# Routed experts in half blocks of two experts side by side, with outputs scattered to a row per choice

## The reference, cut to what matters

```python
def step(y, p):
    w1, b1, w2, b2, w3, b3, ge = p
    h = jax.nn.silu(xt @ w1 + b1) * (xt @ w2 + b2)
    return (y + ge[:, None] * (h @ w3 + b3), None)
y, _ = jax.lax.scan(step, jnp.zeros_like(xt), (ew1, eb1, ew2, eb2, ew3, eb3, gate.T))
z = jax.nn.silu(xt @ sw1 + sb1) * (xt @ sw2 + sb2) @ sw3 + sb3
return (y + z).reshape(shape)
...
x = x + jnp.tanh(g_ffn[0]) * _L0_ffn_ref(_layernorm(x, axis=-1), ...)
```

## Time and profile before

| | us |
|---|---|
| Time, median of 3 runs | 962.04 (961.36 to 962.27) |
| The profiled execution, its own time | 963.37 |
| Its span, first to last instruction | 961.6 |
| PE busy in it | 944.8 |
| DVE busy | 642.8 |
| ACT busy | 410.9 |
| POOL busy | 273.0 |

### The profile page before, as it was taken

The page is one execution under the profiler, slowest core; times in us unless marked ns, Lnnn a source line. Parts: engine busy times, 40 slices in busy tenths (PEclk is TensorE's granted clock), DMA queues, the critical chain, the costliest instruction groups (busy, mean ns, idle before and its releaser), DMA issues.

```text
span 961.6 us, 14022 instructions
## 1 busy us (share of the span) xinstructions
PE 944.8 (98%) x4863; PEld 790.2 (82%) x4863; DVE 642.8 (67%) x1074; ACT 410.9 (43%) x1004; POOL 273.0 (28%) x251
## 2 busy tenths in 40 slices
PE   9999999999999999999999999999999999999996
PEld 7888888888888788888888988989889887777773
DVE  6977679766665864643777778787787777843333
ACT  6336554333333342314556455464554425324442
POOL 1253434433433033003223122121311012043353
PEclk9999999999999999999999999999999999999998
DMA  7654554646456635548747636546465049565579
GB/s 265 223 206 177 187 196 154 229 166 217 174 210 202 217 146 202 202 153 308 262 168 294 225 137 229 197 168 225 138 227 187 39 165 346 197 206 184 171 199 262
DMA packets 86275, 193.75 MB, mean 201 GB/s; under 512 B 8608, under 2 KB 29344, under 8 KB 84800
## 3 DMA queue, kind: packets, MB, share of 16 engines
q1 hardware_dynamic: 76000, 171.64, 50.1%
q0 software_dynamic: 4272, 12.58, 5.0%
q10 hardware_dynamic: 5936, 8.65, 2.5%
HBM read 121.74 MB, written 71.11 MB: 201 GB/s over the span
## 4 chain that ended last, share of the span: by engine, by line
PE 89%; DVE 4%; DMA 2%; issue 2%; POOL 1%; ACT 0%; POOLq 0%; SPq 0%; DVEq 0%; ACTq 0%
PE ps_job L825 7%; PE ps_job L827 7%; PE ps_job L826 7%; PE ps_attn L1041 6%; PE ps_score L1013 6%; PE ps_attn L1285 4%; PE ps_turn L1027 3%; PE ps_score L885 3%; PE ps_score L887 3%; PE ps_score L886 3%; PE ps_attn L885 3%; PE ps_attn L886 3%; PE ps_attn L887 3%; PE ps_job L885 2%; PE ps_job L887 2%; PE ps_job L886 2%
## 5 line engine op out<-in xcount | busy, mean ns | idle before, releaser
L751 POOL TENSOR_TENSOR score_bias<-mask_bias,pos_bias 128x1024 f32<-128x1024 f32 x32 | 78.2, 2445 | 292.0 <-DVE probs L1855 185.9
L1339 ACT ACTIVATE probs<-probs,neg_max 128x128 f32<-128x128 f32 x256 | 99.4, 392 | 95.6 <-DVE neg_max L1858 95.6
L712 POOL TENSOR_TENSOR w_sum<-w_raw 128x256 f32<-128x256 f32 x30 | 22.6, 752 | 178.2 <-PE ps_score L887 72.3
L1041 PE MATMUL ps_attn<-pT,v_s 128*128 128x128 f32 x512 | 62.7, 276 | 1.3 <-issue 1.1
L1285 PE MATMUL ps_attn<-ew_s,xbT 128*128 x248 | 62.4, 380 | 0.9 <-ACT xbT L1329 0.9
L1013 PE MATMUL ps_score<-kq_s 128*128 128x128 f32 x512 | 62.4, 275 | 0.0
L1041 PEld LDWEIGHTS ps_attn<-pT,v_s 128*128 128x128 f32 x512 | 59.8, 192 | 2.0 <-issue 1.2
L1285 PEld LDWEIGHTS ps_attn<-ew_s,xbT 128*128 128x128 f32 x248 | 44.6, 190 | 20.1 <-issue 15.0
L1013 PEld LDWEIGHTS ps_score<-kq_s 128*128 128x128 f32 x512 | 59.9, 192 | 0.2
L1882 DVE TENSOR_TENSOR acc<-ps_job,acc 128x512 f32<-128x512 f32 x56 | 37.9, 685 | 29.9 <-PE ps_job L827 29.9
L783 POOL DMA_INDIRECT xb<-x_rows,token_of x31 | 31.2, 1007 | 84.8 <-ACT y_out L1600 40.2
(11 more groups left out here) (468 smaller groups left out, 2593.8 us busy)
## 6 DMA issues: line engine op xcount, KB each, us to landing
kq<-st SPq DMA_DIRECT2D x32, 1024.0 KB, 4.2
kq_s<-kq SPq DMA_DIRECT2D x64, 512.0 KB, 4.5
v_s<-v_all SPq DMA_DIRECT2D x8, 2048.0 KB, 10.8
w_raw<-wa_dram SPq DMA_DIRECT2D x31, 512.0 KB, 5.6
v_all<-st SPq DMA_DIRECT2D x24, 512.0 KB, 3.7
y_slots<-ones SPq DMA_DIRECT2D x32, 256.0 KB, 4.6
wo_raw<-wo_dram SPq DMA_DIRECT2D x8, 1024.0 KB, 6.9
ew_s<-ew_dram SPq DMA_DIRECT2D x4, 2048.0 KB, 12.6
```

The source lines that it names most:

```text
L751: nc.gpsimd.tensor_tensor(score_bias[:], mask_bias[:], pos_bias[:, i % 2].unsqueeze(1).broadcast_to([P, B, P]), ALU.add).then_inc(bias_rea ...
L1041: last = nc.tensor.matmul(ps_attn[half][:, cols(b)], v_s[g % 2][:, BH * half + b, cols(j)], pT[:, half, cols(b)], start=True, stop=True)
L1339: last = nc.scalar.activation(probs[i % 2][:, half, b], probs[i % 2][:, half, b], ACT.Exp, bias=neg_max[:, i % 2, half, b:b + 1], accum_ou ...
```

## The change

Blocks become pairs of half blocks. Each expert's slots are rounded up to 64 instead of 128. NHB = 47 half blocks can occur at most, so the loop runs NB = 24 times, and the two halves of a pair can belong to two experts. `block_h` makes eight products instead of four: for each chunk, one with 64 of the columns of `xbT` into the PSUM partitions 0 to 63, against `ew12_s`, and one with the other 64 into the partitions 64 to 127, against a copy `w12_b` of the second expert's weights. `block_y` makes two products in the same manner, the second one against a copy `w3_b`. DVE makes both copies (1024 and 512 columns) in every pair, loads two owners, and adds the bias in two instructions of 64 partitions.

PE's order for one b is `turn_x(b + 1)`, `turn_h(b - 2)`, `block_h(b)`, `block_y(b - 2)`; `block_h(b)` waits for `hb_biased` of b - 1, which was b - 2.

The gates leave `x_rows`, and ACT's copy to `y_out` (now 4 buffers) has no scale. POOL scatters each pair to `y_rows` in DRAM by an indirect DMA (`store_y`), to a row for each choice and token, so that SP can read them back by 8 plain loads of 512 KB (`y_back`) once the real pairs are stored. DVE multiplies by the gates in the last sums: 16 instructions of 512 columns in place of 4 adds of 1024. The gates `gate_f` are made by four instructions between `add_shared(1)` and `ended`. The clearing stores go.

```diff
-NB = (TOP * T + E * (P - 1)) // P
-NS = NB + 1
+HB = P // 2
+NHB = (TOP * T + E * (HB - 1)) // HB
+NB = (NHB + 1) // 2
+NS = 32
 XB = 11
+YB = 4
...
+        y_out += [place(f"y_out{n}", [P, D], F32, at_attn + (n - 2 + XB - XB_FIRST) * D * 4) for n in range(2, YB)]
...
+        y_back = place("y_back", [P, B, TOP, D], F32, at_ctx_hi)
+        assert TOP * B * D <= (E // 2) * W12
+        w3_b = [place(f"w3_b{n}", [P, D], F32, at_qk + SH * (2 * W12 + 8) * 4 + n * D * 4) for n in range(2)]
...
+        w12_b = [place(f"w12_b{n}", [P, C, 2 * P], F32, at) for n, at in enumerate((at_rt, at_b3))]
...
+        y_rows = nc.dram_tensor("y_rows", (3 * T + NS * P, D), F32, kind="Internal").ap()
+        y_row_tiles = y_rows[0:4 * T].rearrange("(n q t p) d -> q t p n d", n=TOP, q=2, t=B)[0]
...
-                sp.dma_start(y_slot_blocks[s].rearrange("p (c k) -> p c k", c=C),
-                             ones[:].unsqueeze(1).broadcast_to([P, C, P])).then_inc(cleared, 16)
...
-            sp.wait_ge(gates_out_ready, 1)
-            sp.dma_start(x_rows[:, D:].rearrange("(b p) e -> p b e", p=P), gates_out[:]).then_inc(x_rows_in, 16)
...
+            sp.wait_ge(stores_known, 1)
+            stored_blocks = [sp.value_load(stores_i[0:1, k:k + 1], min_val=HB, max_val=16 * ((NB + YB - 1) // YB))
+                             for k in range(YB)]
+            for k in range(YB):
+                sp.wait_ge(y_stored[k], stored_blocks[k])
             for t in range(B):
-                sp.wait_ge(final_ready, t // 2 + 1)
+                sp.dma_start(y_back[:, t], y_row_tiles[t]).then_inc(y_in[t], 16)
+            for t in range(B):
+                sp.wait_ge(final_ready, t + 1)
                 sp.dma_start(out[t], acc[:, t]).then_inc(stored, 16)
...
-            for b in range(NB):
+            for b in range(XB):
                 if b == XB_FIRST:
                     pool.wait_ge(shared_psum, B)
-                if b >= XB:
-                    pool.wait_ge(yb_sbuf, b - XB + 1)
                 load_x(b)
...
-            pool.wait_ge(stores_known, 1)
-            stores = [pool.value_load(stores_i[0:1, k:k + 1], min_val=P, max_val=16 * NB) for k in range(2)]
-            for k in range(2):
-                pool.wait_ge(y_stored[k], stores[k])
-            nc.gpsimd.tensor_tensor(slot_at[:], base_i[:], row_i[:], ALU.add).then_inc(rank_done, 1)
-            pool.wait_ge(shared_added, B)
-            pool.wait_ge(rank_done, 15)
-            def pick_up(n, t):
+            def store_y(b):
+                if b == 0:
+                    pool.wait_ge(token_ready, 2)
+                pool.wait_ge(yb_sbuf, b + 1)
                 nc.gpsimd.indirect_dma_start(
-                    out=(acc[:, t] if n else y_pick[t // BH][:, t % BH]), out_offset=None, in_=y_slots,
-                    in_offset=bass.IndirectOffsetOnAxis(ap=slot_at[:, n * B + t:n * B + t + 1], axis=0),
-                    bounds_check=NB * P - 1, oob_is_err=True,
-                    compute_op=(ALU.add if n else ALU.bypass)).then_inc(y_pick_in[t], 16)
-            for t in range(B):
-                for n in range(TOP):
-                    pick_up(n, t)
+                    out=y_rows, out_offset=bass.IndirectOffsetOnAxis(ap=row_of[:, b:b + 1], axis=0),
+                    in_=y_out[b % YB][:], in_offset=None,
+                    bounds_check=3 * T + NS * P - 1, oob_is_err=False).then_inc(y_stored[b % YB], 16)
...
-            def block_h(b, e, chunks):
+                return pe.value_load(owner[0:1, 2 * b:2 * b + 1], min_val=0, max_val=E - 1)
+            def block_h(b, e):
                 k = b % 2
-                for c in chunks:
-                    last = nc.tensor.matmul(ps_attn[k][:, 0:2 * P], xbT[k][:, cols(c)], ew12_s[:, e, c],
-                                            start=(c == 0), stop=(c == C - 1))
-                return last
+                for c in range(C):
+                    for half, w in enumerate((ew12_s[:, e, c], w12_b[k][:, c])):
+                        last = nc.tensor.matmul(ps_attn[k][half * HB:(half + 1) * HB, 0:2 * P], xbT[k][:, cols(2 * c + half, HB)],
+                                                w, start=(c == 0), stop=(c == C - 1))
+                last.then_inc(hb_psum, 1)
             def block_y(b, e):
                 k = b % 2
                 pe.wait_ge(hbT_sbuf, b + 1)
                 if b >= 2:
                     pe.wait_ge(yb_sbuf, b - 1)
-                nc.tensor.matmul(ps_job[k][:], hT_b[k][:], w3_s[:, e], start=True, stop=True).then_inc(yb_psum, 1)
+                for half, w in enumerate((w3_s[:, e], w3_b[k][:])):
+                    last = nc.tensor.matmul(ps_job[k][half * HB:(half + 1) * HB, :], hT_b[k][:, cols(half, HB)], w,
+                                            start=True, stop=True)
+                last.then_inc(yb_psum, 1)
...
-            turn_x(1)
             pe.wait_ge(shared_added, B)
-            owners = [owner_of(0)]
-            for b in range(NB):
-                pe.wait_ge(xbT_sbuf, b + 1)
+            owners = []
+            for b in range(NB + 2):
+                if b + 1 < NB:
+                    turn_x(b + 1)
                 if b >= 2:
-                    pe.wait_ge(hb_biased, b - 1)
-                if b == 0:
-                    block_h(b, owners[b], range(C)).then_inc(hb_psum, 1)
-                else:
-                    block_h(b, owners[b], range(2))
-                    turn_h(b - 1)
-                    block_h(b, owners[b], range(2, C)).then_inc(hb_psum, 1)
-                if b + 1 < NB:
-                    owners.append(owner_of(b + 1))
-                if b + 2 < NB:
-                    turn_x(b + 2)
-                if b == 1:
+                    turn_h(b - 2)
+                if b < NB:
+                    owners.append(owner_of(b))
+                    pe.wait_ge(xbT_sbuf, b + 1)
+                    if b >= 1:
+                        pe.wait_ge(hb_biased, b)
+                    block_h(b, owners[b])
+                if b == 2:
                     pe.wait_ge(ew3_in, 16 * 4)
-                if b >= 1:
-                    block_y(b - 1, owners[b - 1])
-            turn_h(NB - 1)
-            block_y(NB - 1, owners[NB - 1])
+                if b >= 2:
+                    block_y(b - 2, owners[b - 2])
...
+                if b >= YB:
+                    act.wait_ge(y_stored[b % YB], 16 * (b // YB))
+                copy(y_out[b % YB][:], ps_job[k][:]).then_inc(yb_sbuf, 1)
+            take_xbT(0)
+            for b in range(NB + 2):
+                if b + 1 < NB:
+                    take_xbT(b + 1)
+                if b < NB:
+                    k = b % 2
+                    act.wait_ge(hb_biased, b + 1)
+                    nc.scalar.activation(silu_b[k][:], h_b[k][:, 0:P], ACT.Silu).then_inc(silu_b_done, 1)
                 if b >= 2:
-                    act.wait_ge(y_stored[k], 16 * (b // 2))
-                nc.scalar.activation(y_out[k][:], ps_job[k][:], ACT.Copy,
-                                     scale=xb[b % XB][:, bass.ds(owners[b] + D, 1)]).then_inc(yb_sbuf, 1)
-                if b == 0:
-                    act.wait_ge(cleared, 16 * NS)
-                act.wait_ge(yb_sbuf, b + 1)
-                act.dma_start(y_slot_blocks[b], y_out[k][:]).then_inc(y_stored[k], 16)
-            def owner_of(b):
-                return act.value_load(owner[0:1, b:b + 1], min_val=0, max_val=E - 1)
-            take_xbT(0)
-            take_xbT(1)
-            act.wait_ge(owner_ready, 1)
-            owners = [owner_of(0)]
-            for b in range(NB):
-                k = b % 2
-                act.wait_ge(hb_biased, b + 1)
-                nc.scalar.activation(silu_b[k][:], h_b[k][:, 0:P], ACT.Silu).then_inc(silu_b_done, 1)
-                if b + 2 < NB:
-                    take_xbT(b + 2)
-                if b >= 1:
-                    take_y(b - 1)
-                if b + 1 < NB:
-                    owners.append(owner_of(b + 1))
-            take_y(NB - 1)
+                    take_y(b - 2)
...
-            dve.wait_ge(gain_done, 1)
-            V.scalar_tensor_tensor(out=gates_out[:], in0=masks[:], scalar=gain[:, 1:2], in1=scores[:],
-                                   op0=ALU.mult, op1=ALU.mult).then_inc(gates_out_ready, 1)
...
+            chain(V.tensor_scalar(blocks_i[:], ps_score[1][:, B * E:(B + 1) * E], float(HB - 1), None, ALU.add))
+            chain(V.tensor_scalar(blocks_i[:], blocks_i[:], HB.bit_length() - 1, None, ALU.arith_shift_right))
...
-            V.tensor_scalar(base_i[:], slot_i[:], -P, None, ALU.bitwise_and)
...
-            V.tensor_copy(token_of[:], ps_turn[1][:, 0:NS]).then_inc(token_ready, 1)
+            chain(V.tensor_copy(row_of[:], ps_turn[1][:, 0:NS]))
+            V.tensor_scalar(token_of[:], row_of[:], T - 1, None, ALU.bitwise_and).then_inc(token_ready, 1)
+            chain(V.scalar_tensor_tensor(out=spare[:], in0=ps_turn[1][:, 0:NS], scalar=0.0, in1=spare[:],
```

(62 more changed lines are left out.)

104 lines of the change are left out of this document (50 added, 54 removed).

## The result

The changed kernel took 955.81 us (median of four runs, 955.19 to 956.83), the kernel before 961.94 beside it: a ratio of 0.9938, with a 95% interval of 0.9921 to 0.9955. A second set gave 0.9944 (0.993 to 0.9958), 959.31 against 964.46.

What follows compares the result with a forecast made beforehand. The prediction took PE to bound the old loop and DVE the new one: first `h_b` 858.5 + pairs 81.7 + 0.8 + slow loads 2.7 + 2.55 + sums 11.2 + ending 2.9 = 960.3 profiled, 960.7 as median; range 948 to 977.

Steps and rivals of the forecast that it cites:

- 23 pairs: Loop after the first `h_b`: each pair takes 3.55 us, set by DVE, 81.7 us in all.
- slow loads in the ending: About pairs 21 and 22: four owner loads slowed by plain-load DMA traffic, some 0.7 us extra each, +2.7 us.
- last `h_b`, drain: End of loop: last bias 0.8 us, then DVE's remaining work before the sums, 2.55 us.
- part 3: Before the loop: `gate_f`, longer `ended` and `owner_f`, and first copies move the first `block_h` from 854.37 to 856.5, +2.1 us.
- part 1: PE in the loop: 24 pairs replace 31 blocks, both halves run at once, so a pair needs 3.14 us.
- the serial rival: `block_h` and `block_y`: halves run one after the other, PE needs 5.71 us a pair, total 1009; chance 0.17.
- part 2: DVE in the loop: owner loads, copies, two biases and handoffs sum to 3.5 us a pair, taken as 3.55.
- The bound moves from PE to DVE: Loop: DVE's 3.55 us a pair exceeds PE's 3.14, so 24 pairs cost 85 us, not 75.
- the third rival: Loop: DVE's owner loads hide, a pair takes PE's 3.14 to 3.3 us, total 948 to 952; chance 0.22.
- The collision: Loop: DVE's loads and copies collide with POOL's scatter, a pair takes 4.0 to 4.2 us, total 970 to 975; chance 0.21.
- break-even: Loop: if DVE and POOL collide, the changed kernel loses from a pair of 3.63 us on.
- part 4: Ending: 2.55 us on DVE, 16 sums of 11.2 (+6.6 on the path), last store and end 2.9; plain loads hidden.

Runs made afterwards that it cites:

- the shared ending: Changed kernel with owner loads made a pair ahead, plus two of the eight last tiles multiplied by ScalarE and added by POOL: 957.34 us, 0.9945 to the kernel before.

## Why the prediction was right, and where not

The forecast of 960.7 was 4.9 us above the result. Its mechanism stood (most of what PE saves is spent on DVE, so little is left), but not its size: 1.3 us were forecast and 6.1 measured, and its chances gave slower (0.47) more than faster (0.38). By its own sum, on the profiled spans (960.3 forecast, 954.5 measured):

| term | forecast | measured | difference |
|---|---|---|---|
| first `h_b` starts | 858.5 | 856.95 | -1.55 |
| 23 pairs | 81.7 | 79.74 | -1.96 |
| slow loads in the ending | 2.7 | in the 79.74 | -2.7 |
| last `h_b`, drain | 0.8 + 2.55 | 0.85 + 2.72 | +0.2 |
| 16 sums | 11.2 | 11.68 | +0.5 |
| last store and end | 2.9 | 2.52 | -0.4 |

The measured column is one profile. In the second one of the same kernel the first `h_b` starts at 858.44 and the 23 pairs take 81.55, 1.8 of it the late `h_b` of pair 1, so that its span (957.8) is 2.5 below the forecast and not 5.8.

- *The start (part 3).* The steps were right: `gate_f` 1.4, `ended` and `owner_f` 0.95 and 0.94, `add_shared(2)` 4.8 behind the first shared add. What was off is the first shared add itself: 843.60 in this profile, 844.93 in the kernel before. That belongs to the execution, not to the change: of the fourteen profiles of this study it lies at 843.4 to 844.0 in five and at 844.9 to 845.9 in nine, with the kernels mixed in both. In the second profile of the changed kernel it was 845.07, and there the forecast fits: `add_shared(2)` 849.88 (849.7), first `block_h` 856.34 (856.5), first `h_b` 858.44 (858.5). 1.3 us of the 7.1 between the first two profiles are therefore not the change's.
- *PE's share (part 1).* Both halves at once: right, and the serial rival fell. The pair of 3.14 was wrong by 0.3, for the two changes of tiling, each 0.15. The step that failed here is that they were named and left out of the sum. That it cost nothing is luck: DVE's own pair, 3.42, happened to be just as long and hid it. The Trainium skill, TensorEngine Tiling (Array Packing), Key Properties, gives both rules, that tiles work in parallel and that changing the mode drains the engine; the runs agree with both, and put 0.15 us on the second. 
- *DVE's share (part 2).* 3.42 measured against 3.55 taken, each step within 0.2 us: `copy_w12` began at G + 1.58 (1.75), since a load with its check took 0.63, not 0.65, and the first began at G + 0.24. "The bound moves from PE to DVE" is half right: the chain does run through DVE, but PE's own work is just as long, 3.43. Each was hidden by the other, so taking the loads away bought 1.5 us at most, and the third rival, loads that hide and a pair of 3.14 to 3.3, could not come true: PE didn't allow it until the changes of tiling were halved.
- *Slow loads.* Mis-sized: four at 0.7 us extra, 2.7 in all, were forecast, and one slow load of 0.705 was seen, 0.4 extra. The earlier trace rows had loads up to 1.381 beside 16 pick-ups that POOL issued. Here only the last three owner loads fell beside the plain ones, for those were issued when the loop was nearly over (first line), and of these three (0.298, 0.705, 0.298) one was slow, as in the second profile (0.562). So the stretch was met by fewer loads than forecast; whether plain loads disturb less than pick-ups isn't shown by so few.

```profile
L689 SPq DMA_DIRECT2D y_back<-y_rows x8: 370/520/2757, 928.2 to 934.5; - x8
...
L2120 DVEq TENSOR_LOAD <-owner x48: 298/300/705, 849.5 to 932.1; - x48
```

- *The collision.* Its condition (a POOL instruction beside `copy_w12`) came true in every pair, its effect didn't: `copy_w12` took 0.69 in 20 of 24 (0.87 at most), POOL's scatter 1.14 at the median instead of the 0.98 that it takes beside no copy. The break-even that goes with it is off by a little, too: by the sum's own 1.3 us it lies at a pair of 3.61, not 3.63. The argument against it was the right one: the earlier trace rows show a POOL tensor instruction, and an indirect DMA is another thing. With tensor adds on POOL the collision came at once, in the shared ending. The Trainium skill, SBUF — State Buffer, Who interferes with whom, says that a VectorE instruction with two inputs in SBUF contends with a GpSimd instruction that reads SBUF; the four sums of 1.63 to 2.02 agree. Its rule for copies in the mode with two ports, that copy and GpSimd instruction exclude each other for their whole length, isn't borne out for an indirect DMA: in the rows above `copy_w12` (890.89 to 891.58) runs in the midst of a scatter (890.56 to 891.70), and neither waited for the other to end. Here the measurement decides.
- *The ending (part 4).* Sums, drain and hidden loads as forecast: `y_back` landed from 933.6 on, 6.7 us ahead of the first sum.

## What to carry to other kernels

Count every switch between full and part tiles of the array as a price of its own (0.15 us here), and order the work so that operations of one tiling stand together: with the owner loads out of the way, that took a pair from 3.43 to 3.28. Two engines whose chains are equally long hide each other; taking work from one shows nothing, so work out both before saying which one bounds. Before a share of the last sums goes to GpSimd, ask how many of VectorE's operands lie in SBUF: the helper may cost more than it takes.

## What the runs showed of the hardware that was not expected

- Half products that alternate start within 0.01 us of each other, and PE overlapped halves that stood some four records apart: in turn instead of alternating, a pair of 4.35 instead of 3.43.
- A change of tiling costs 0.14 to 0.20 us, the same for two half products behind it as for sixteen.
- The order of POOL's scatter and gather moved the start of a VectorE instruction by up to 2 us in each group (ratios of 1.0023 against 0.9905, some 11 us), though none of the three waits for the others in the program. VectorE started 0.14 behind PE's semaphore as always; it was the semaphore that rose 1.6 to 2.4 us behind the modelled end of PE's product, and why is open.
- The shared adds before the loop begin in one of two ranges (843.4 to 844.0 or 844.9 to 845.9) from one execution to the next, with the same kernel in both (843.60 and 845.07). One profile against one other can't tell a change of 1.5 us from that.
